# Feed-forward layers that sort their tokens by expert through device memory and compute only the two chosen experts

## The reference

```
x = x + 0.5 * ffn(layernorm(x));  x = x + attention(layernorm(x));  x = x + 0.5 * ffn(layernorm(x))

# ffn: 8 experts, each token goes to 2 of them, and a shared expert sees every token
scores = softmax(x @ router_w)
_, sel = top_k(scores + expert_bias, 2)
out = swiglu(x, sw1, sw2, sw3) + sum over the 2 chosen e of scores[e] * swiglu(x, w1[e], w2[e], w3[e])
# swiglu(x, w1, w2, w3) = (silu(x @ w1) * (x @ w3)) @ w2, all matrices 128 x 128
```

## Time and profile before

| | |
|---|---|
| median of 3 runs | 1352.4 us (1349.47 to 1357.5) |
| profiled execution | 1349.75 us, its span 1348.0 us |
| PE busy | 1238.0 us, 92% of the span, 11940 matmuls |
| DVE, ACT, POOL busy | 82%, 62%, 41% |
| granted TensorE clock, mean | 0.973 of full speed |

### The profile page before, as it was taken

How to read it: one execution, slowest core, us unless ns; L and a number is a source line. 1 busy time by engine, 2 the same in 40 slices (tenths; PEclk the granted TensorE clock), 3 DMA queues, 4 the chain that set the end, 5 groups by cost and what they waited for, 6 DMA issues and landing times. The chain is left out here.

```text
span 1348.0 us, 34907 instructions
## 1 busy us (share of the span) xinstructions
PE 1238.0 (92%) x11940; PEld 691.8 (51%) x11940; DVE 1107.1 (82%) x2686; ACT 833.5 (62%) x1477; POOL 554.5 (41%) x658
## 2 busy tenths in 40 slices
PE   5999999999979999999999999899899999999998
PEld 2555555555533555555555555555455555555554
DVE  6888888888975688888888888888688898988876
ACT  5665565656543566666666666666565656566564
POOL 3454544544530233333333333333354554554444
PEclk9999999999995799999999999999899999999999
DMA  6000000000000000000000000000000000000000
GB/s 186 2 1 1 0 0 0 0 0 0 1 1 1 1 1 2 2 2 2 2 2 2 1 2 2 1 2 2 2 2 16 9 16 8 16 8 16 8 9 25
DMA packets 21417, 11.85 MB, mean 9 GB/s; under 512 B 960, under 2 KB 21312, under 8 KB 21312
## 3 DMA queue, kind: packets, MB, share of 16 engines
q1 hardware_dynamic: 21312, 10.43, 2.8%
HBM read 6.23 MB, written 4.19 MB: 8 GB/s over the span
## 5 line engine op out<-in xcount | busy, mean ns | idle before, releaser
L672 POOL TENSOR_TENSOR h_lo<-h,h_hi 128x512 f16<-128x512 f32 x288 | 337.7, 1173 | 386.3 <-ACT h_hi L634 375.6
L1109 DVE TENSOR_REDUCE neg_max_at<-score_at 128x2 f16<-128x512 f32 (+1 forms) x384 | 254.4, 692 | 78.1 <-PE score_at L940 72.5
L1229 POOL TENSOR_SCALAR_AFFINE_SELECT probs_at<-probs_at 128x512 f32<-128x512 f32 x256 | 157.0, 637 | 352.4 <-ACT probs_at L1187 351.9
L634 ACT ACTIVATE h_hi<-h 128x512 f16<-128x512 f32 x288 | 180.6, 627 | 152.7 <-DVE h L435 150.8
L1187 ACT ACTIVATE probs_at<-prob_at 128x512 f32<-128x512 f32 x384 | 201.6, 598 | 79.3 <-PE prob_at L972 77.4
L435 DVE TENSOR_TENSOR h<-prod,gate_b 128x512 f32<-128x512 f32 x256 | 174.9, 683 | 53.9 <-PE gate_b L543 53.7
L564 PE MATMUL y_b<-w_hi,h_hi 128*128 128x128 f16 x1152 | 207.8, 219 | 2.6 <-POOL h_lo L672 2.6
L564 PE MATMUL y_b<-w_hi,h_lo 128*128 128x128 f16 x1152 | 207.8, 219 | 0.0
L564 PE MATMUL y_b<-w_lo,h_hi 128*128 128x128 f16 x1152 | 207.8, 219 | 0.0
L429 DVE TENSOR_TENSOR prod<-silu,b 128x512 f32<-128x512 f32 x256 | 175.5, 686 | 37.9 <-ACT silu L623 23.6
L623 ACT ACTIVATE silu<-a 128x512 f32<-128x512 f32 x288 | 169.7, 589 | 49.7 <-PE a L530 48.3
(11 more groups left out here) (138 smaller groups left out, 2203.4 us busy)
## 6 DMA issues: line engine op xcount, KB each, us to landing
x<-in_L_attn_x_dram SPq DMA_DIRECT2D x16, 256.0 KB, 3.0
out_dram<-x SPq DMA_DIRECT2D x16, 256.0 KB, 2.3
raw_w<-in_L_ffn_w_dram SPq DMA_DIRECT2D x3, 512.0 KB, 5.2
raw_w<-in_L_ffn_sw_dram SPq DMA_DIRECT2D x3, 64.0 KB, 4.1
raw_attn<-in_L_attn_W_Q_dram SPq DMA_DIRECT2D x1, 64.0 KB, 4.9
raw_attn<-in_L_attn_W_K_dram SPq DMA_DIRECT2D x1, 64.0 KB, 3.6
raw_attn<-in_L_attn_W_V_dram SPq DMA_DIRECT2D x1, 64.0 KB, 3.6
raw_attn<-in_L_attn_W_O_dram SPq DMA_DIRECT2D x1, 64.0 KB, 3.7
```

Source lines behind the costliest of these rows:

```text
L634: nc.scalar.activation(h_hi[k][:, :], h[k][:, :], ACT.Copy).then_inc(hhi_done, 1)
L672: nc.gpsimd.tensor_tensor(h_lo[k][:, :], h[k][:, :], h_hi[k][:, :], ALU.subtract).then_inc(hlo_done, 1)
L1109: nc.vector.tensor_reduce(dst, src, AX.X, ALU.max, negate=True).then_inc(max_done, 1)
L1229: nc.gpsimd.affine_select(out=p, in_=p, compare_op=ALU.is_ge, fill=0.0, base=0, pattern=[[0, GROUPS], [1, P]], channel_multiplier=-1).then ...
```

## The change

In `ffn_phase` the eight routed experts are no longer computed for every token. The block is now 56 iterations in one numbering. The first 16 are the chunks, each with the shared expert alone. The tokens are then handled in four quarters of four chunks. For a quarter, DVE works out in 32 instructions on 128x128 elements (`gates(b)`, of which some have 128x256) which two experts each token takes and at which row it stands when the quarter's 4096 token copies are sorted by expert, each expert's rows padded to whole parts of 128 (40 parts). PE's `rank(b)` counts with 32 small matmuls for it. POOL writes the normalised tokens to those rows in device memory by indirect DMAs of 128 rows of 512 bytes (`scatter`: 32 for each quarter, 128 for each layer). SP loads four parts at a time (`load`: 256 KB). Iterations 16 to 55 are these 40 rounds, ten for each quarter. In a round each part has its own expert: PE reads its number from memory into a register (`value_load`) and addresses the weights by it, so that all matmuls are 128 columns wide. ACT copies `y` out (`copy_y`), SP stores it (`store`). At the end POOL fetches each token's two rows back (`fetch`: 8 indirect DMAs for each chunk, 128 for each layer) and DVE's `combine` adds them with their gates. POOL's `h_lo` is now DVE's (`low_h`). There are 20 further stores of zeros to device memory ahead of phase 0's scatter (`blank_rows`). The norms of attention's first two chunks are made at the start of attention. `run_pairs`, a loop in registers over pairs of chunks, is gone; all is written out.

```diff
...
-LAG = 3
+LAG = 2
...
+QUARTERS = 4
+QUARTER = CHUNKS // QUARTERS
+BATCH = QUARTER * TILES
+PARTS = 2 * BATCH + EXPERTS
+ROUNDS = PARTS // TILES
...
+    def blank_rows(self, sp, rows):
+        self.wait_pool_tables(sp)
+        for q in range(QUARTERS):
+            for i in range(PARTS // (2 * TILES)):
+                some = rows["in"][q][i * 2 * TILES * P:(i + 1) * 2 * TILES * P, :]
+                sp.dma_start(some.rearrange("(p t) d -> p t d", p=P),
+                             self.consts["blank"][:, :, :]).then_inc(self.blanked[q], DMA)
...
+LOADS, STORES, BACKS = 4, 3, 3
+STORE_LAG = 7
+GATE_PLACES = (2, 2, 2, 4, 6, 8, 10, 12, 14, 16, 18, 20, 22, 24, 26, 28, 30, 32, 32, 32, 32)
+POINTS = 5
+PICKED, PLACED = 18, 29
+GATE_STEPS = 32
+ITERATIONS = CHUNKS + QUARTERS * ROUNDS
...
+            def load(i):
+                q, j = divmod(i, ROUNDS)
+                if j == 0:
+                    sp.wait_ge(scattered[q], 2 * BATCH * DMA)
+                if i >= LOADS:
+                    sp.wait_ge(xt_done, CHUNKS + i - LOADS + 1)
+                sp.dma_start(row_in[i % LOADS][:, :, :],
+                             round_rows(rows["in"][q], j)).then_inc(row_loaded[i % LOADS], DMA)
+            def store(i):
+                q, j = divmod(i, ROUNDS)
+                sp.wait_ge(y_copied, i + 1)
+                sp.dma_start(round_rows(rows["out"][q], j),
+                             row_out[i % STORES][:, :, :]).then_inc(row_stored[i % STORES], DMA)
+            for i in range(QUARTERS * ROUNDS):
+                load(i)
+                if i >= STORE_LAG:
+                    store(i - STORE_LAG)
...
+            def combine(c):
+                dve.wait_ge(fetched[c % BACKS], (c // BACKS + 1) * 2 * TILES * DMA)
+                dve.wait_ge(x_added, c + 1)
+                for k in range(2):
+                    for t in range(TILES):
+                        tile = x[:, c * TILES + t, :]
+                        at = c * TILES + t
+                        last = nc.vector.scalar_tensor_tensor(tile, back[c % BACKS][:, 2 * t + k, :],
+                                                              gate[:, k, at:at + 1], tile, ALU.mult, ALU.add)
+                    last.then_inc(combined if k else first_added, 1)
+                    if k == 0:
+                        dve.wait_ge(first_added, c + 1)
...
+            for n in range(ITERATIONS):
+                product(n)
+                beside(n, 0)
+                if n + 2 < ITERATIONS:
+                    split_x(n + 2)
+                beside(n, 1)
+                low_h(n)
+                beside(n, 2)
+                if is_chunk(n + 3):
+                    scale(n + 3)
+                beside(n, 3)
+                if n >= LAG and is_chunk(n - LAG):
+                    residual(n - LAG)
+                if is_chunk(n + 4):
+                    norm(n + 4)
+                beside(n, 4)
+                if prepare and n == 1:
+                    prepare.low(dve, nc.vector, "attn", y_bank[1])
+                if prepare and n == CHUNKS + 8:
+                    select_heads(nc, consts, prepare.dve_tables)
+            for c in range(CHUNKS):
+                combine(c)
...
+            def weight(name, n, k):
+                if is_chunk(n):
+                    return w[name][:, 0, :]
+                return w[name][:, bass.ds(part_expert[n, k], 1), :].rearrange("p a d -> p (a d)")
...
+            def up(n):
+                pe.wait_ge(xhi_done, n + 1)
+                pe.wait_ge(xlo_done, n + 1)
+                parts = (slice(0, CHUNK),)
+                if not is_chunk(n):
+                    q, j = divmod(n - CHUNKS, ROUNDS)
+                    if j == 0:
+                        pe.wait_ge(gate_step, (q + 1) * GATE_STEPS)
+                    parts = [slice(k * P, (k + 1) * P) for k in range(TILES)]
+                    for k in range(TILES):
+                        part_expert[n, k] = pe.value_load(expert[q][0:1, TILES * j + k:TILES * j + k + 1], min_val=1,
+                                                          max_val=EXPERTS)
...
+                    for k, part in enumerate(parts):
+                        pairs = ((name + "_hi", xt_hi), (name + "_lo", xt_hi), (name + "_hi", xt_lo))
+                        for i, (ws, xs) in enumerate(pairs):
+                            last = nc.tensor.matmul(dst[:, part], weight(ws, n, k), xs[n % 2][:, part],
+                                                    start=(i == 0), stop=(i == 2))
                     last.then_inc(done, 1)
...
+            def copy_y(n):
+                i = n - CHUNKS
+                act.wait_ge(w2_done, n + 1)
+                if i >= STORES:
+                    act.wait_ge(row_stored[i % STORES], i // STORES * DMA)
+                nc.scalar.activation(row_out[i % STORES][:, :, :],
+                                     y_bank[n % 2][:, :].rearrange("p (t d) -> p t d", d=P),
+                                     ACT.Copy).then_inc(y_copied, 1)
...
-                nc.gpsimd.tensor_tensor(h_lo[k][:, :], h[k][:, :], h_hi[k][:, :], ALU.subtract).then_inc(hlo_done, 1)
...
+            def scatter(tile):
+                q = tile // BATCH
+                pool.wait_ge(gate_step, q * GATE_STEPS + PLACED)
+                if prepare and tile % BATCH == 0:
+                    prepare.wait_blank(pool, q)
+                for k in range(2):
+                    nc.gpsimd.indirect_dma_start(rows["in"][q][:, :],
+                                                 bass.IndirectOffsetOnAxis(place[:, k, tile:tile + 1], 0),
+                                                 xn[:, tile, :], None).then_inc(scattered[q], DMA)
+            def fetch(c):
+                q = c // QUARTER
+                if c % QUARTER == 0:
+                    for s in range(STORES):
+                        pool.wait_ge(row_stored[s], len(range(s, (q + 1) * ROUNDS, STORES)) * DMA)
+                if c >= BACKS:
+                    pool.wait_ge(combined, c - BACKS + 1)
+                for t in range(TILES):
+                    at = c * TILES + t
+                    for k in range(2):
+                        nc.gpsimd.indirect_dma_start(back[c % BACKS][:, 2 * t + k, :], None, rows["out"][q][:, :],
+                                                     bass.IndirectOffsetOnAxis(place[:, k, at:at + 1], 0)
+                                                     ).then_inc(fetched[c % BACKS], DMA)
...
+            for c in range(CHUNKS):
+                norm_root(pool, nc, c, buf, ln_step, ln_rooted)
+                if prepare and c == 1:
+                    prepare.low(pool, nc.gpsimd, "w2")
+                if c >= 11:
+                    for tile in range(3 * (c - 11), 3 * (c - 10)):
+                        scatter(tile)
+            for tile in range(3 * (CHUNKS - 11), CHUNKS * TILES):
+                scatter(tile)
+            for c in range(CHUNKS):
+                fetch(c)
...```

Three places in the order of the instructions. First PE's: before, a step of phase 0 ended with the last matmuls of `down` and went on with `up` and the gate's matmul.

```order
160 L564 MATMUL y_b_0<-w_hi,h_hi_0 128x128
161 L564 MATMUL y_b_0<-w_hi,h_lo_0 128x128
162 L530 MATMUL a_0<-xt_hi,w_hi 128x512
163 L530 MATMUL a_0<-xt_hi,w_lo 128x512
164 L530 MATMUL a_0<-xt_lo,w_hi 128x512
165 L543 MATMUL gate_b<-gate_t_0,select_gate 128x512
166 L530 MATMUL b_0<-xt_hi,w_hi 128x512
```

More of the change, by code:

```diff
@@ L262, in ffn_phase @@
         h_lo = [sb(f"h_lo{s}", [P, CHUNK], F16) for s in range(3)]
[L263 to L269, removed]
@@ new lines, in ffn_phase @@
+        chosen = sb("chosen", [P, 2, BATCH, EXPERTS], F32)
+        both = sb("both", [P, 2, BATCH, EXPERTS], F32)
+        picked = sb("picked", [P, BATCH, EXPERTS], F16)
+        place_f = sb("place_f", [P, 2, BATCH], F32)
+        place = sb("place", [P, 2, CHUNKS * TILES], U32)
+        gate = sb("gate", [P, 2, CHUNKS * TILES], F32)
+        tab = {n: sb(n, [P, EXPERTS], F32) for n in ("parts_of", "last_part", "first_part")}
+        above = sb("above", [P, EXPERTS, BATCH], F32)
+        summed = sb("summed", [P, EXPERTS, EXPERTS], F32)
@@ L408, in gates, with beside @@
                     done.then_inc(gate_step, 1)
-            def beside(c, e, place):
-                first, last = GATE_PLACES[2 * e + place], GATE_PLACES[2 * e + place + 1]
-                if not is_last(c):
-                    gates(c + 1, first, last)
-            def swiglu(c, slot, e):
-                n, k = c * STEPS + e, (slot + e) % 2
+            def beside(n, point):
+                b, since = gate_time(n)
+                at = since * POINTS + point
+                if point == POINTS - 1 and is_chunk(n) and n % 4 == 3:
+                    gates(n // 4, 0, 2)
+                if b is not None:
+                    gates(b, GATE_PLACES[at], GATE_PLACES[at + 1])
@@ L419, in swiglu, with product @@
+            def product(n):
                 dve.wait_ge(silu_done, n + 1)
@@ L444, in chunk @@
```

(42 more changed lines are left out.)

512 lines of the change are left out of this document (260 added, 252 removed).

## The result

The changed kernel took 1577.6 us (median of 4, 1574.21 to 1587.23) beside 1350.93 before (4 runs, 1345.75 to 1357.5): ratio 1.1686, 95% interval 1.1613 to 1.176. It is slower, as forecast, by 227 us and not 368. Two later measurements of the same file, on two chips (which chip the first ran on is not on record), gave 1853 and 1860 us, while the kernel before stayed at 1352 and 1350 there. Most of what follows is about these two facts: terms of the sum that were too large, and a cost that the sum did not have at all.

The account below looks back on a forecast made before the run. Chunks by DVE, rounds by PE's queue at half clock, then POOL's tail were taken to bound it: 520 + 291 - 443 = +368 us, 1718, against the median 1720; own range 1600 to 1850, whole range 1480 to 1970.

Parts of the forecast that it names:

- 334 + 80 r + 208 p - 777: Whole kernel: new layers and attention's 8 us, less the old layers' 777 us; forecast change +368 us.
- r: Time of one of a layer's 40 rounds, by PE and its queue: 6.5 us, bounds 2.5 and 9.8.
- p: POOL's time for each indirect DMA: 1.4 us, between 0.43 and 3.0; 104 fetches exposed in a layer's tail.
- the 159 and 149 in the 334: Ends of the 16 chunks in the two layers, in us: 139 for the chunks plus starts of 20 and 10.
- The wait for POOL's roots: Chunks from 11 on: DVE's `scale` waits for a root behind six scatters, 9.7 against 7.5 us, five times: 11.
- I take half clock: Rounds: PE at half clock, 36 matmuls and four transposes 4.7 us; at full clock 2.5.
- its 7.6 us for a round: Rounds: the skill's `tensor_load` floor, none hidden: 4.7 + 2.4 + 0.5 us, making the forecast 88 us higher.
- I take 0.5 us: Rounds: the 32 register and `ISA` rows of a round, for which no profile row was found, cost 0.5 us.
- The 8 us: Attention's start: two norms, roots, scales and a transpose, no longer prepared, come ahead of its first products: 8 us.
- (2): Rounds and tail: loads and register rows hidden, fetches cheap, r 4.7, p 1.2: +183, 1535 us; chance 0.18.
- (4): POOL's indirect DMAs are dear, p = 2.3: +555, 1905 us, most of it the tail; chance 0.17.
- The scatters themselves are hidden: Scatters on POOL: 98 left at chunk 12 take 137 us, within the 225 before quarter 3 starts.

Follow-up runs that it names:

- c2: Changed kernel with only the first of each token's two experts fetched and combined, 64 fetches a layer for 128: 1700.8 us beside the unchanged one's 1852.8.
- c3: Changed kernel with each fetch and combine covering partitions 0 to 63 only, same number of DMA instructions: 1860.4 us beside the unchanged one's 1852.8.
- e4: Changed kernel with twelve buffers for fetched rows in place of three, nothing else: 1842.1 us.
- c1: The changed kernel once more, not a line different, on a second chip: 1852.8 us (1846.8 to 1866.4).
- g2: Changed kernel with one load for four expert numbers, twelve buffers and a GpSimd power between every six indirect DMAs: 1692.9 us beside the unchanged one's 1860.0.
- d2: Changed kernel with a GpSimd power of 128 x 4 elements before every fourth indirect DMA: 1651.5 us, unchanged kernel not timed beside it.
- four sound experiments: Changed kernel without expert loads on PE, with constant weight addresses, with one load for four values, with twelve buffers: 1629.8, 1731.7, 1784.8 and 1842.1 us.
- a fifth and sixth: Changed kernel with GpSimd, before every fourth indirect DMA, waiting for all earlier ones to land, or computing a power: 1701.2 and 1651.5 us.

## Why the prediction was right and wrong

The direction was right and by the right parts: the matmul work is gone, and chunks on DVE, rounds on PE's queue and a tail on POOL stand in its place. The formula 334 + 80 r + 208 p - 777 is borne out with measured values: r = 5.9 and p = 1.25 give 334 + 472 + 260 - 777 = +289; the chunks ended 23 and 27 us earlier than the 159 and 149 in the 334, and attention took 7 less of its 8; that leaves +232, and the spans differ by 228. By its number the first measurement lies outside the forecast's own range of 1600 to 1850 us, 142 under the 1720, and the later two just above that range; that all three are slower and inside the whole range is the width of the range, not the sum.

- **Chunks.** Sized too high: they end at 135.8 and 121.8 us for 159 and 149. The starts were right, 19.1 and 9.6 us for 20 and 10, so the 16 chunks take 117 and 112 us for 139, with DVE busy 94 and 93 of them. Most of the 22 us is the choice of experts. The sum had eight gate instructions of it in every chunk, 43 us, but a quarter's choice can begin only behind its chunks, so that of the last quarter stands beside the rounds; 98 instructions of 28.3 us fall into the first layer's chunks. Three of each kind ran by 133 us, as in the first line below. The wait for POOL's roots was 2.4 us from 27 on and not 11, while DVE waited 11.7 us for ACT's `xt_hi`, which the sum did not have, and PE 9.8 us for the first rows.

```profile
L486 DVE TENSOR_REDUCE gate<-both 128x32 f32<-128x256 f32 x3 | 1.3, 420 | 0.1
L101 DVE TENSOR_SCALAR xn<-x,moments,rstd 128x128 f32<-128x128 f32 x52 | 14.8, 351 | 2.4 <-POOL rstd L94 2.4
L403 DVE TENSOR_TENSOR xt_lo<-xt,xt_hi 128x512 f16<-128x512 f32 x15 | 10.3, 683 | 11.7 <-ACT xt_hi L740 11.7
```

- **Rounds.** 5.9 us for 6.5, but by errors that cancel. "I take half clock" failed: the clock was 0.85, and the work of a round is 2.45 us at full clock (2.5 had been named as the lower bound), not 4.7. The loads, 1.3 us exposed, measured 1.5. (By the floor of about 600 ns that the Trainium skill, "DMA: Bandwidth & Descriptors", Latency and other measured facts, gives `tensor_load`, four are 2.4 us; their spacing of 0.67 us agrees with it, and part of them is hidden, by which its 7.6 us for a round did not come.) The register rows, "I take 0.5 us", are the step that failed worst: with what they do to the clock they cost 1.9. What was said to refute the forecast, a clock of 1.00, did not come either; it moved between the two levels.
- **Tail.** p was 1.25 for 1.4, so 137 and 140 us for 155; that it is POOL's issue, exposed by three buffers, is shown by c2, c3 and e4.
- **Attention.** The 8 us came where they were put: DVE's first `q_pack_at` starts 17.3 us into attention for 7.9 before. Yet attention took 572.0 us for 570.6. It no longer prepares the second layer's first norms; whether that paid the 8 us back was not tested.
- **The rivals.** (2), the cheap one, gave 1535, 43 us under the first measurement, and so is much nearer to it than the forecast; its p of 1.2 was nearly right, but its reason for the rounds, hidden loads, is wrong. (4) was wrong in its mechanism, yet 1853 and 1860 us are near its 1905, for a reason nobody had.
- **What was missing.** "The scatters themselves are hidden" holds for the first measurement only. In the two others, PE all but stands still beside POOL's indirect DMAs though it waits for nothing of POOL's, and the kernel takes 275 and 282 us more. Of the 270 us by which c1's span is longer, 129 and 132 are the two layers and 9 attention. The sum had a price for POOL's time and for the transfers, none for what they do to PE's instruction flow. Both levels lie within the forecast range, so the range hid this gap.

The cause of the stalls stays open: why the first measurement had none at the same spacing; which resource it is, since the DMA share is 0.16 in the stalled window and the landing times of POOL's DMAs are missing from every trace with stalls; whether PE is slowed in taking instructions or in reporting their ends. The recording itself is not excluded: every execution here has a recorded span and clock, and the stalled ones lack events. That the rate of indirect DMAs decides, rather than the longest row of them, rests on four spacings, with two other edits in two of them and the last one measured at another time.

Could another version beat the kernel before? 256 indirect DMAs at 1.25 us are 320 us of POOL for a layer. The first starts at 77 us; with 7 for the end that is 404 us, against 396 before. In the second layer the first starts 63 us in (1143.91, where attention's last matmul is at 1080.92; the 86 in g2's expectation is wrong), so 63 + 320 + 7 = 390 against 381. The roots between the scatters, some 7 us a layer, come on top.

```profile
1143.91 1.06 POOL L801 DMA_INDIRECT in_rows<-xn,place  x1 [0.18 <-issue]
```

So even without stalls the layers would be 17 us or more behind, and at d2's 1.6 us they are 494 and 480. These are sums and were not run. Apart from the first measurement, the best version that computes the whole result is d2 with 1651.5 us, 1.222 times the kernel before (1.217 to 1.227).

## What to carry to other kernels

Count the indirect DMAs of a plan by instruction, not by byte: here each moved 128 rows at most and held GpSimd 1.25 us, so 256 of them are 320 us of its time in a layer, and of the edits only c2, with fewer, shortened its queue by more than 2%. Cost run-time addresses twice, once for the load that stands in the queue and once for the arithmetic among short matmuls. Before reading small edits, time the unchanged kernel beside them, each time: four sound experiments looked like failures, most likely because their base had moved from 1578 to about 1855 us, and a fifth and sixth that looked like a cure cannot be told from a base that had moved back.

## What the hardware showed

- Beside rows of indirect DMAs started 1.26 us apart, on three chips, PE began one instruction per 0.7 to 1.4 us, and DVE and ACT waited up to 40 us. One earlier measurement at the same spacing had none of it. With an addition of 0.2 us between every four DMAs 64 matmuls ran in 40 us for 34, with a power of 1.05 us between every six 174.
- An indirect DMA costs GpSimd 0.95 us and 0.30 between two, with 64 rows 0.91 us for the 0.95.
- Reading an expert number from SBUF on PE's sequencer: a row of 0.30 us, 0.67 us from one to the next, 3.2 us of PE standing still for four. The Trainium skill ("Runtime: NRT & Kernel Launch", The ~15µs preamble/postamble breakdown) tells of `TENSOR_LOAD` rows of about 1.3 us when they read device memory; here they read SBUF and are shorter.
